# A two-layer graph network on one core: layer norm moments and attention shares taken per batch of tiles, eight more edge groups unrolled on VectorE

## What is computed

```
h  = max(layernorm(x), 0)
m  = silu(silu([h[src], h[dst], edge_attr, w / 5] @ ew1 + eb1) @ ew2 + eb2)
agg = segment_sum(m, src)
x1 = x + h + silu([h, agg] @ nw1 + nb1) @ nw2 + nb2
h1 = max(layernorm(x1), 0)
for W, a_src, a_dst, b, heads, ch in ((W1, .., 4, 32), (W2, .., 1, 64)):
    t = h1 @ W                                   # [n, heads, ch]
    s, d = sum(t * a_src, -1), sum(t * a_dst, -1)
    e = leaky_relu(s[src] + d[dst], 0.2)
    h1 = segment_sum(t[src] * segment_softmax(e, dst), dst) + b
    (after the first layer: h1 = relu(h1))
out = x1 + h1
```

## Time and profile before

| | us |
|---|---|
| Median of 3 runs | 8928.67 (8913.6 to 8929.7) |
| Profiled execution, its own time | 8916.15 |
| Its span, first to last instruction | 8914.5 |
| DVE busy | 6392.5 (72%) |
| PE busy | 6375.9 (72%) |
| GpSimd busy | 6136.1 (69%) |
| ACT busy | 4848.8 (54%) |

### The profile page before, as it was taken

How to read it: one execution, slowest core, us unless ns; L and a number is a source line. 1 busy time by engine, 2 the same in 40 slices (tenths; PEclk the granted TensorE clock), 3 DMA queues, 4 the chain that set the end, 5 groups by cost and what they waited for, 6 DMA issues and landing times.

```text
span 8914.5 us, 232214 instructions
## 1 busy us (share of the span) xinstructions
PE 6375.9 (72%) x50562; PEld 5197.4 (58%) x50563; DVE 6392.5 (72%) x27688; ACT 4848.8 (54%) x11854; POOL 6136.1 (69%) x7562
## 2 busy tenths in 40 slices
PE   2466666666599999985777777777647777777775
PEld 2366656665588888863444444444445665556664
DVE  7799833333267767757999999999957777777776
ACT  4133333333245555535767667677647777777775
POOL 0377777777777777735777777777637777777775
PEclk9988888888799999986888888888755555555555
DMA  4232222222233333312222222222521111111114
GB/s 141 52 63 62 62 63 62 63 62 62 60 92 85 86 86 85 86 30 59 55 54 55 54 54 55 55 54 54 49 23 28 28 28 28 28 28 28 28 28 27
DMA packets 990660, 491.49 MB, mean 55 GB/s; under 512 B 830674, under 2 KB 841604, under 8 KB 990276
## 3 DMA queue, kind: packets, MB, share of 16 engines
q0 software_dynamic: 168832, 302.29, 15.6%
q1 hardware_dynamic: 701892, 169.48, 10.4%
q10 hardware_dynamic: 119840, 18.68, 1.3%
HBM read 356.53 MB, written 151.48 MB: 57 GB/s over the span
## 4 chain that ended last, share of the span: by engine, by line
issue 25%; DVE 20%; PE 19%; POOL 18%; DMA 7%; ACT 6%; DVEq 3%; ACTq 1%; POOLq 0%; SPq 0%
POOL z_s L637 13%; POOL arena L687 5%; DMA arena<-table,arena 5%; PE ps_all L959 5%; PE ps_all L969 5%; PE ps_all L982 3%; ACT arena L823 3%; PE ps_all L979 2%; DVE shift L1528 2%; DVE arena L1487 2%; DVE arena L1532 2%; PE ps_all L1066 1%; ACT arena L855 1%; DVE arena L1573 1%; DMA z_s<-arena 1%
## 5 line engine op out<-in xcount | busy, mean ns | idle before, releaser
L687 POOL DMA_INDIRECT arena<-table,arena x3616 | 3471.7, 960 | 1504.4 <-issue 982.6
L637 POOL DMA_INDIRECT z_s<-arena x1660 | 1592.1, 959 | 849.9 <-issue 477.5
L1090 PE MATMUL ps_all<-arena 128*128 128x132 f32 (+1 forms) x7232 | 1561.4, 384 | 1.8 <-DVE acc L1590 1.8
L1090 PEld LDWEIGHTS ps_all<-arena 128*128 128x128 f32 x7232 | 1384.9, 284 | 2.7 <-issue 2.6
L823 ACT ACTIVATE arena<-lanes_b,arena 128x128 bf16<-128x128 bf16 x3616 | 1147.1, 387 | 415.6 <-DVE arena L1461 414.4
L1487 DVE TENSOR_REDUCE arena<-ps_all 128x2 f32<-128x1024 f32 x904 | 1098.9, 1216 | 15.5 <-PE ps_all L1107 15.5
L1066 PE MATMUL ps_all<-ident_b,arena 128*128 128x128 bf16 x3616 | 472.3, 273 | 789.1 <-DMA arena<-table,arena 522.6
L1107 PE MATMUL ps_all<-arena,pick 128*128 128x512 bf16 x2260 | 971.0, 523 | 72.5 <-DVE arena L1487 72.1
L847 ACT ACTIVATE arena<-ps_all 28x512 bf16<-28x512 bf16 (+1 forms) x904 | 522.6, 578 | 718.5 <-PE ps_all L1066 718.5
L742 ACT ACTIVATE arena<-ps_all 18x512 f32<-18x512 f32 x415 | 243.3, 586 | 1212.0 <-PE ps_all L946 1192.5
L1066 PEld LDWEIGHTS ps_all<-ident_b,arena 128*128 128x128 bf16 x3616 | 291.1, 120 | 942.7 <-DVE arena L1474 528.8
(11 more groups left out here) (259 smaller groups left out, 16141.0 us busy)
## 6 DMA issues: line engine op xcount, KB each, us to landing
arena<-z_s SPq DMA_DIRECT2D x452, 264.0 KB, 2.7
arena<-table,arena POOLq DMA_INDIRECT x3616
arena<-rec_d SPq DMA_DIRECT2D x1660, 10.0 KB
z_s<-arena POOLq DMA_INDIRECT x1660
rec_d<-in_rec ACTq DMA_DIRECT2D x1, 16160.0 KB, 58.8
arena<-ids_d SPq DMA_DIRECT2D x904, 4.0 KB
arena<-pos_d SPq DMA_DIRECT2D x830, 0.5 KB
arena<-pos_d ACTq DMA_DIRECT2D x830, 0.5 KB
```

The source lines that it names most:

```text
L637: pool.indirect_dma_start(z_s, bass.IndirectOffsetOnAxis(ap=slot[:, g.slot(SLOTS), u:u + 1], axis=0), z_out[:, g.slot(SLOTS), u, :], None) ...
L687: pool.indirect_dma_start(g_rows[:, r, u * step + CODE_WORDS:(u + 1) * step], None, tables[n], bass.IndirectOffsetOnAxis(ap=ids[:, r, 0, u ...
L1090: mm = pe.matmul(ps[6][:, 0:out_w], a_hot_f[:, g.slot(4), u, :], g_msg[:, g.slot(4), u * out_w:(u + 1) * out_w], start=(u == 0), stop=(u = ...
```

## The change

Three edits, all on DVE:

1. `layer_norm` is split into `moments(tiles)` (sum, mean, difference, square, sum of squares) and `normed(which)` (the rest). The second layer norm's moments are taken for each batch right after its update was added, inside the loop over PE's batches.
2. In the table of a layer the products with the attention vectors and the sums over a head are taken for each batch right after its copy. The sums of all heads are one instruction with four dimensions.
3. The edge perceptron's pipeline on DVE writes out 24 steps ahead of its loop in place of 16. The loop is as long as before and runs 53 turns in place of 54.

```
-            def layer_norm(which):
...
-                link(dve.tensor_reduce(stat[:, 0, :], xs, op=ALU.add, axis=AX.X))
...
-                link(dve.tensor_reduce(stat[:, 1, :], sq, op=ALU.add, axis=AX.X))
+            def moments(tiles):
+
+                n = len(tiles)
+                at = slice(tiles[0], tiles[0] + n)
+                link(dve.tensor_reduce(stat[:, 0, at], xs[:, at], op=ALU.add, axis=AX.X))
+                link(dve.tensor_scalar(stat[:, 0, at], stat[:, 0, at], 1.0 / F_IN, None, ALU.mult))
+                link(dve.tensor_tensor(hs[:, at], xs[:, at], stat[:, 0, at].unsqueeze(2).broadcast_to([P, n, F_IN]), ALU.subtract))
+                link(dve.tensor_tensor(sq[:, at], hs[:, at], hs[:, at], ALU.mult))
+                link(dve.tensor_reduce(stat[:, 1, at], sq[:, at], op=ALU.add, axis=AX.X))
+
+            def normed(which):
                 link(dve.tensor_scalar(stat[:, 1, :], stat[:, 1, :], 1.0 / F_IN, 1e-5, ALU.mult, ALU.add))
...
-            edge_pipeline(dve, GROUPS, 6, edge_mlp, src_buckets.load, peel=2 * SLOTS)
+            edge_pipeline(dve, GROUPS, 6, edge_mlp, src_buckets.load, peel=3 * SLOTS)
...
                 dve.tensor_tensor(to, to, ps[6 + b % 2][:, 0:len(tiles) * F_IN], ALU.add).then_inc(S("node_added"), 1)
-            dve.wait_ge(S("node_added"), len(BATCHES))
-            layer_norm(1)
+                dve.wait_ge(S("node_added"), b + 1)
+                dve.wait_ge(S("node_t"), b + 1)
+                moments(tiles)
+            normed(1)
...
-                dve.wait_ge(S("gat_copied"), before + len(BATCHES))
-                for vec, to in ((att_s[n], a_s), (att_d[n], a_d)):
-                    link(dve.tensor_tensor(plain, tb[:, :, at_f:row], vec.unsqueeze(1).broadcast_to([P, NT, width]), ALU.mult))
-                    for h in range(heads):
-                        link(dve.tensor_reduce(to[:, :, h], plain[:, :, h * ch:(h + 1) * ch], op=ALU.add, axis=AX.X))
+                    dve.wait_ge(S("gat_copied"), before + b + 1)
+                    dve.wait_ge(S("gat_t"), before + b + 1)
+                    at, m = slice(tiles[0], tiles[0] + len(tiles)), len(tiles)
+                    for vec, to in ((att_s[n], a_s), (att_d[n], a_d)):
+                        link(dve.tensor_tensor(plain[:, at], tb[:, at, at_f:row], vec.unsqueeze(1).broadcast_to([P, m, width]), ALU.mult))
+                        link(dve.tensor_reduce(to[:, at], plain[:, at].rearrange("p t (h c) -> p t h c", h=heads), op=ALU.add, axis=AX.X))
```

More of the change, by code:

```diff
@@ L1116, in _ @@
             link(dve.memset(zero, 0.0))
-            def layer_norm(which):
-                if which == 0:
-                    dve.wait_ge(S("x_in"), 16)
-                link(dve.tensor_reduce(stat[:, 0, :], xs, op=ALU.add, axis=AX.X))
[L1123 to L1126, removed]
-                link(dve.tensor_reduce(stat[:, 1, :], sq, op=ALU.add, axis=AX.X))
+            sq = tab[:, 0:NT * F_IN].rearrange("p (t f) -> p t f", t=NT)
+            def moments(tiles):
[7 more added lines that the diff above has]
+            def normed(which):
                 link(dve.tensor_scalar(stat[:, 1, :], stat[:, 1, :], 1.0 / F_IN, 1e-5, ALU.mult, ALU.add))
@@ L1133, in layer_norm @@
                 link(dve.tensor_scalar(hs, hs, 0.0, None, ALU.max))
-            layer_norm(0)
+            dve.wait_ge(S("x_in"), 16)
+            moments(range(NT))
+            normed(0)
             dve.sem_inc(S("h_ready"), 1)
```

## The result

| | before | changed |
|---|---|---|
| Median, 11 runs each on one chip | 8928.67 us (8913.6 to 8933.6) | 8906.01 us (8901.4 to 8910.0) |
| Ratio | | 0.9977, 95% interval 0.9969 to 0.9986 |
| Profiled execution: own time, span | 8916.15, 8914.5 | 8909.09, 8906.0 |
| On a second chip, 15 and 11 runs | 8919.84 | 8899.21; 0.9977 (0.9968 to 0.9986) |

The change makes the kernel 22.7 us faster, and 20.6 on the second chip; 29.8 were forecast, and the time forecast, 8899, is 7 us too low. In the gain the forecast is outside both intervals, which run from 12.5 to 27.7 us and from 12.5 to 28.5. What follows shows that the miss is the sum of steps that came out within 1 us and of two that did not.

A forecast was written before the change was run, and what follows sets the result against it. No engine bounds the whole; the edited stretches run one after another, each with one engine at work. Terms -10.1 - 15.2 - 5.8 + 1.3 = -29.8 us from the median 8928.67 give 8898.9; range for 8 in 10: 8878 to 8922.

The forecast's parts named there:

- Moments, 10.1: Second layer norm: moments taken per batch, 2.5 us hidden in PE's 3.91 us batch spacing; gain 10.1 us.
- First table, 15.2: First layer's table: DVE becomes the bound at 3.7 us a batch, ending at 4013.8; gain 15.2 us.
- Second table, 5.8: Second layer's table: DVE follows PE for seven batches, then is the bound at 2.3 us a batch; gain 5.8 us.
- until the copy at 6522.42, then every 1.7 to 1.3, when its clock rises: Second table: PE delivers batches every 2.45 us up to that copy, then every 1.7 to 1.3 us.
- Eight more steps, 1.3: Edge perceptron: eight more steps written out, each 0.16 us longer than in the loop; loss 1.3 us.
- The attention stretches as long as before, and no instruction packet in them: Sign expected in the profile after: both attention layers unchanged in length, with no instruction fetch in them.
- rival 1: Attention loops: DVE's program no longer stays on hand; slower overall from 0.55 us a turn on; chance 0.10.
- begin at unlike places: Argument against refetching: attention loops of 356 and 351 instructions, starting at different places, both ran without a packet.
- Second and third rival: Linked short instructions cost more, gain 5.7, time 8923 us, chance 0.10; PE's clock stays up, 8882 us, chance 0.1.

The follow-up runs named there:

- edit_1_placed: Kernel before with the first edit alone and 42 tiny DVE memsets behind the first layer's table: 12260.52 us, 6.6 less than before on a slow chip.
- one_memset: Kernel before with one tiny DVE memset behind the first layer's table, on a slow chip: 12297.34 against 12267.12 us, ratio 1.0023.
- one_memset_b: Kernel before with one tiny DVE memset behind the first layer's table, on another slow chip: 12045.78 against 12017.13 us, ratio 1.0024.
- second_placed: Changed kernel with 70 tiny DVE memsets behind the second layer's table only; loops begin at 12 and 29: 8896.09 us, ratio 0.9978.
- both_placed: Changed kernel with 15 and 54 tiny DVE memsets behind the two layers' tables; loops begin at 28 and 29: 8890.28 us, ratio 0.9970.
- changed_third: Changed kernel run again without edits, on a chip where the kernel before took 8919.84 us: 8899.21 us, ratio 0.9977.
- no_edit_3: Changed kernel with its third edit undone (16 steps written out), no memsets; loops begin at 52 and 126: 9055.89 us, ratio 1.0156.

## Why the prediction came out as it did

**Moments, 10.1: right.** 10.1 in every profile that has them, batch by batch as worked out (2.45 us for 2.5, idle 1.46 for 1.4).

**First table, 15.2: right, 1.0 too low.** A batch takes 3.62 and not 3.7: the look at a second semaphore costs nothing that shows. 45.1 us for 46.1.

**Second table, 5.8: right for the profile shown, too large as a mean.** The step that failed is "until the copy at 6522.42, then every 1.7 to 1.3, when its clock rises": it took the moment of the rise as a property of the kernel, but it is one of the execution. In the old order the stage took 35.7, 29.9, 33.3, 30.0 and 31.0 us in five profiles (the last three those of edit_1_placed, one_memset and one_memset_b), in the new one 29.2 to 29.8 in the six profiles of the table above, since DVE's pace hides when PE speeds up. The gain is 0 to 6, 2.3 in the mean of the five.

**Eight more steps, 1.3: right, 0.3 too low.** 1429.5 against 1427.9 us, 1.6.

**"The attention stretches as long as before, and no instruction packet in them": wrong.** This is the step with the largest share in the 7 us.
- In the first layer the loop's turn is 42.23 to 42.29 us in three profiles with the loop at 12, and 42.10 to 42.14 in four with it at 28: 0.13 a turn, 7 us in 54 turns; by the stages 2487.4 against 2480.1 in the mean, 7.3. second_placed against both_placed shows 5.8 in the time itself. That it is the place follows from these. How it acts is argued from records only: in the changed kernel the turn grows by about 0.1 us at each of the two borders within the loop (behind its 116th and 244th instruction), while at the borders of the kernel before (behind the 100th and 228th) nothing comparable is seen, so whether DVE's chain feels a border may depend on what stands there. The prediction had no term for a loop that fits.
- In the second layer rival 1 came true, and at its price: DVE is stopped 2.6 us at the end of each turn (2.7 was taken from a load that lands after that time), 267 packets more move. As worked out there, POOL's pace hides it, though perhaps not in whole: turns of 40.45 to 40.53 against 40.33 to 40.39, 0.13 in the mean, of which a third to a half is the first turn alone and is made up behind the loop; by the stages 2 us, with values that overlap (2373.8 to 2377.4 against 2371.1 to 2374.6); in the whole time of second_placed against changed_third nothing that can be told across chips.
- The price of rival 1 in the first layer was 146 us (9045). no_edit_3 shows 168 in the stage: right in kind, low by the 0.3 us at each passage. It was given 0.10. The change misses it only because the third edit puts the first loop at 12 in place of 52, and that was luck: the prediction says that this edit chooses the place, but works out no place.
- The chance of 0.10 leaned on two loops of the kernel before that "begin at unlike places" and both ran without a packet. They begin at 28 and 29 of a piece, so they were one observation and not two. By the limit found here a loop of 356 instructions fits from 29 of 128 places only; for a loop moved to an unknown place, a fetch in each turn was the likelier outcome.

Put together: -10.1 - 16.2 + 1.6 + 7.3 + 2 = -15.4, and 0 to 6 more for the second table, so 15 to 21 us faster. The two measurements say 22.7 and 20.6, with intervals that begin at 12.5, so the stages and the times agree. The forecast of 29.8 is above both intervals, by 2.1 and 1.3 us. That it is no further off is luck in two places: the second loop came to be fetched anew in each turn where POOL's pace hides it, and the first did not.

The Trainium skill, Runtime: NRT & Kernel Launch, section Instruction fetch mechanics, was cited in the prediction for a window of two pages of 256 instructions. On the mechanism the trace agrees: a branch back to code that is no longer on hand waits for a fetch, 2.4 to 3.8 us in the loops here. On the size it does not. The pieces of 128 that the trace shows can be paired into pages of 256 in two ways. By the one, the first loop of one_memset touches only two pages, by the other the second loop of the changed kernel does; yet both were fetched anew each turn, so neither way fits, and the measurement decides. By the runs here a loop on DVE stays on hand in three pieces of 128 and not in four.

**Second and third rival.** Linked short instructions did not cost more (3.62 us a batch where 4.3 would have told so), and PE's clock did not stay up: 0.50 in the first table as before.

## What to carry to other kernels

A loop of hand-written code has a place as well as a length. When an edit adds instructions anywhere ahead of a long loop, count from the built program how many 8 KB packets the loop touches, and look at the instruction queue in the profile after: packets inside a steady loop mean that it is fetched each turn, whatever the busy times say. Where a loop is near the limit, fix its place with instructions in a stretch where the engine waits anyway; here that, with the third edit left out (1.6 us), was worth 7.6 us beside the change's 20.6. With the third edit left out and no place fixed the same kernel is 140 us slower than before.
Work that is taken off an engine-after-engine stretch shows in full and to the tenth in that stretch. The few per mille of the whole need stages cut at the same instructions, and the turn of a loop in two or more profiles, since one profile against another carries 6 us of other differences here. A run of the kernel that one suspects, with the place alone changed, is worth more than either.

## What was not expected of the hardware

- DVE's code is on hand for three packets of 128 instructions (8 KB each). A loop that touches four moves about five packets a turn (267 in 54 turns) and stops at the branch back: 2.4 to 2.6 us with the loop at 52 or 86 of a piece, 3.6 to 3.8 with it at 30 or 126, where it ends two instructions behind a border or begins two ahead of one.
- Two instructions decide it: a first loop at 28 of a piece shows no packet, at 30 it shows 265 more.
- Within three pieces, the place of a loop still changed its turn by 0.13 us in 42.1.
- PE's clock rose behind the second copy of the second table in one execution and behind the seventh in another, of one and the same kernel, 6 us of difference in that stage.
- On two chips all kernels took 12.0 to 12.3 ms, with the perceptron, norm and first table as long as on the others. The gathers' packets in the attention layers began 1.65 us after the instruction and ended 2.2 us after it, there as on the other chips (median of each). What DVE and POOL wait for in the attention stages of these chips stays open.
